# Moving the issue of a small on-chip copy from SyncE's queue to ScalarE's

## The reference, cut to what matters

```
scores = q @ k.T * scale                # per head, 256 x 256, some with a mask or a window
attn   = softmax(scores)                # needs the maximum of each query's scores
out    = attn @ v
```

## Time and profile before

| what | value |
|---|---|
| time, 3 runs | 2492.68 us median (2490.92 to 2495.97) |
| profiled execution | 2494.33 us, of which 2492.2 us is the span |
| granted TensorE clock over the span | 0.983 |
| PE busy | 2363.5 us, 95% of the span |
| ACT busy | 1120.0 us, 45% |
| DVE / POOL busy | 1568.9 us / 517.7 us |

### The profile page before, as it was taken

How to read it: one execution, slowest core, us unless ns; L and a number is a source line. 1 busy time by engine, 2 the same in 40 slices (tenths; PEclk the granted TensorE clock), 3 DMA queues, 4 the chain that set the end, 5 groups by cost and what they waited for, 6 DMA issues and landing times.

```text
span 2492.2 us, 49538 instructions
## 1 busy us (share of the span) xinstructions
PE 2363.5 (95%) x18862; PEld 1745.2 (70%) x18862; DVE 1568.9 (63%) x2673; ACT 1120.0 (45%) x1761; POOL 517.7 (21%) x1120
## 2 busy tenths in 40 slices
PE   6999999999998999999999999999999999999976
PEld 4777777777776676777767677777777677777654
DVE  6757576666757657466675676666665757576422
ACT  3344445544444535435353544444453544545422
POOL 4211113222212222121113122111222212121100
PEclk9999999999999999999999999999999999999987
DMA  7412122321211132212111331121222312211100
GB/s 214 149 39 61 41 64 63 92 64 51 70 49 48 50 83 67 71 53 70 44 53 53 92 85 50 40 74 53 66 71 60 79 48 62 57 49 40 39 18 22
DMA packets 164233, 159.13 MB, mean 64 GB/s; under 512 B 17824, under 2 KB 162720, under 8 KB 162976
## 3 DMA queue, kind: packets, MB, share of 16 engines
q1 hardware_dynamic: 164000, 155.97, 22.9%
HBM read 35.71 MB, written 4.19 MB: 16 GB/s over the span
## 4 chain that ended last, share of the span: by engine, by line
PE 71%; issue 12%; DVE 8%; ACT 3%; DVEq 2%; POOL 2%; POOLq 1%; SPq 1%; DMA 1%; ACTq 0%
PE work L1078 17%; PE work L1069 13%; PE unit L1139 8%; PE out L1161 7%; PE unit L1111 7%; PE unit L1107 5%; PE unit L1135 4%; DVE neg_max L954 4%; PE work L1060 3%; PE work L1276 2%; ACT probs L739 1%; PE unit L1131 1%; PE work L1306 1%; DVE hidden_t L974 1%; DVEq L873 1%
## 5 line engine op out<-in xcount | busy, mean ns | idle before, releaser
L954 DVE TENSOR_REDUCE neg_max<-unit 128x4 f32<-128x1024 f32 (+1 forms) x640 | 727.2, 1163 | 286.6 <-PE unit L1111 281.5
L739 ACT ACTIVATE probs<-unit 128x1024 f32<-128x1024 f32 (+1 forms) x640 | 606.8, 980 | 474.1 <-PE unit L1139 471.2
L1078 PE MATMUL work<-par,hidden_t 128*128 128x256 f32 x1792 | 416.8, 382 | 5.3 <-ACT hidden_t L694 2.2
L1111 PE MATMUL unit<-key_stack,query_stack 96*128 96x256 bf16 x2048 | 350.8, 276 | 23.1 <-issue 8.2
L1078 PEld LDWEIGHTS work<-par,hidden_t 128*128 128x128 f32 x1792 | 332.1, 190 | 55.3 <-ACT hidden_t L694 4.8
L1139 PE MATMUL unit<-query_stack,key_stack 99*128 99x256 bf16 x2048 | 345.7, 276 | 11.0 <-ACT probs L739 4.3
L1069 PE MATMUL work<-tok_t,par 128*128 128x256 f32 x1408 | 335.6, 386 | 3.0 <-ACT tok_t L694 1.9
L1111 PEld LDWEIGHTS unit<-key_stack,query_stack 96*128 96x128 bf16 x2048 | 191.9, 99 | 142.4 <-DVE neg_max L954 23.1
L1069 PEld LDWEIGHTS work<-tok_t,par 128*128 128x128 f32 x1408 | 260.8, 193 | 40.8 <-ACT tok_t L694 4.5
L1161 PE MATMUL out<-probs,values 128*17 128x256 f32 x4096 | 269.2, 386 | 1.2 <-ACT probs L739 1.1
L1139 PEld LDWEIGHTS unit<-query_stack,key_stack 99*128 99x128 bf16 x2048 | 192.5, 98 | 73.9 <-ACT probs L739 14.6
(11 more groups left out here) (163 smaller groups left out, 3293.7 us busy)
## 6 DMA issues: line engine op xcount, KB each, us to landing
query_stack<-query_pieces SPq DMA_DIRECT2D x480, 128.0 KB, 2.4
key_stack<-key_pieces SPq DMA_DIRECT2D x384, 128.0 KB, 2.4
tok_t<-in_x_features SPq DMA_DIRECT2D x16, 256.0 KB, 2.7
c_in<-in_ctx SPq DMA_DIRECT2D x16, 256.0 KB, 3.0
ctx_t<-in_ctx_features SPq DMA_DIRECT2D x16, 256.0 KB, 3.0
x_in<-in_x SPq DMA_DIRECT2D x16, 256.0 KB, 3.2
m_in<-in_mask_self SPq DMA_DIRECT2D x16, 256.0 KB, 3.1
m_in<-in_mask_cross SPq DMA_DIRECT2D x16, 256.0 KB, 3.1
```

The source lines that it names most:

```text
L739: a_.activation(probs[:, n % PROB_BUFS, :, :, 0:width(l)], bank[:, :, :, 0:width(l)], ACT.Exp, scale=SCALE[l]).then_inc(exped, 1)
L954: v.tensor_reduce(neg_max[:, n % HALVES, :, 2 * (u % 4):2 * (u % 4) + 2], bank[:, :, :, 0:width(l)], AX.X, ALU.max, negate=True).then_inc( ...
L1078: last = pe.matmul(bank[:, t, :], src[:, t * P:(t + 1) * P], weight, start=(n == 0), stop=(n == len(parts) - 1))
L1111: last = pe.matmul(bank[:, t, i, 0:n], queries[0:ROWS, h, t * P:(t + 1) * P], keys[0:ROWS, 0 if l == "l2" else h, columns(l, t)], start=ma ...
```

## The change

The `turn` branch of SP's walk is taken out, and the same wait and the same transfer are put into ACT's walk, right behind the cast. The order of the steps is as it was.

```diff
@@ SP's walk
                     if step in ("ksplit", "qsplit"):
                         split(key)
-                    elif step in ("turn0", "turn1"):
-                        n = TURN_NO.place[key]
-                        a = int(step[-1])
-                        wait_taken(sp, key)
-                        sp.dma_start(query_buffer(b, l)[ROWS:MAX_ROWS, HC * a:HC * (a + 1), :],
-                                     max_rows[:, n % 2, :]).then_inc(max_placed[n % 2], 16)
                     elif step == "loadc":
@@ ACT's walk
                         if n >= 2:
                             act.wait_ge(max_placed[n % 2], 16 * (n // 2))
                         a_.copy(max_rows[:, n % 2, :], bank[0:3 * HC, 0, :]).then_inc(taken, 1)
+                        a = int(step[-1])
+                        wait_taken(act, key)
+                        act.dma_start(query_buffer(b, l)[ROWS:MAX_ROWS, HC * a:HC * (a + 1), :],
+                                      max_rows[:, n % 2, :]).then_inc(max_placed[n % 2], 16)
                     elif step == "out0":
```

## The result

The changed kernel takes 2514.6 us (median of 4 runs, 2513.0 to 2515.0) against 2492.4 us before: a ratio of 1.0086, 95% interval 1.0068 to 1.0103, so +22 us (17 to 26). The forecast was 2524 us with a range of 2500 to 2550. In a later comparison the same kernel stood at 1.0085 (1.0072 to 1.0099).

A forecast was written before the change was run, and what follows sets the result against it. PE was taken to bound the kernel, busy for 2363.5 of 2492.2 us. The terms -6 - 1 + 39 - 4 + 2 = +30 us, on the profiled 2494.3 us, gave 2524 us, range 2500 to 2550.

The forecast's parts named there:

- Direction and mechanism: Whole kernel slower: ACT held 0.6 to 1.0 us per issue, half of it on PE; chance 0.65, range 2508 to 2540.
- The price per place: ACT behind each of 160 casts: next instruction 0.85 us after the cast's end, 0.94 us against an overlapped start.
- Signs that were named: Expected in the new trace: ACT issue near 0.74 us, PE's waits for ACT up some 30 us, PE busy near 2363.
- Late copies, -6 and -1 us: SP's queue: copies no longer issued late behind splits gain PE 6 us; splits behind a copy starting earlier gain 1 us.
- What reaches PE, +39 us: ACT's lateness followed to PE's first dependent instruction: 65 of 160 places reach PE by over 0.1 us, 39 us in all.
- the give-back: Part of PE's lateness is recovered where PE later waits for DVE or POOL anyway: -4 us, between 0 and -15.
- Two issuers at once, +2 us: At 41 places ACT might queue behind SP at the shared descriptor generator: 0 to 26 us of ACT's time, +2 us booked.
- The sum: Whole kernel: -6 - 1 + 39 - 4 + 2 = +30 us.
- a cheap issue: Rival: the issue holds ACT under 0.2 us and late copies come home, giving 2486 us; chance 0.07.
- slack that hides all: Rival: gaps on ACT, busy only 45%, take up nearly all of the 39 us, giving 2494 us; chance 0.08.
- a queue behind SP: Rival: ACT queues behind SP's transfers or its issue takes longer than SP's, giving 2537 to 2550 us; chance 0.20.

The follow-up runs named there:

- the extra transfer: Kernel before, SP issuing the real copies, plus an unneeded 12 KB transfer by ACT behind each cast, scratch laid out as the query stack: 1.0090, repeated 1.0095.
- the 65 places: Against the kernel before, ACT issues the copy only at 65 of 160 places where its lateness was read to reach PE; SP issues the rest: 1.0088.
- the other 95: Against the kernel before, ACT issues the copy only at the 95 places where PE was read as not reached; SP issues the rest: 0.9994.
- the first experiment: Kernel before, plus an unneeded 12 KB transfer by ACT behind each cast to plain contiguous scratch rows, issue 0.296 us: 1.0031, +7.7 us.

## Why the prediction was right, and which terms were not

**Direction and mechanism: right.** ACT's issue holds its sequencer as long as SP's; nothing hides it where ACT's next work is ready; PE is not reached at most places. The extra transfer shows it with SP's side left as it was.

**The price per place: right.** 0.85 us was worked out from SP's rows, 0.86 measured at 757.50, and 0.80 to 0.86 at the other places where ACT's next instruction is ready.

**Signs that were named.** ACT's issue has a row of 0.73 us, the exponential at 755 comes 0.86 us behind the cast, PE's wait there is 1.29 us, the copy at 240 is issued 0.03 us behind the cast, and a copy from ACT lands no later: all as forecast. Two signs missed. PE's idle time that ends with ACT grew by 13.2 us and not by some 30, and PE's busy time rose by 7.4 us instead of staying near 2363.

**Late copies, -6 and -1 us: too large.** About -3, an estimate. The term was added up from PE's waits, the smaller of wait and lateness at nine places. The waits went away as forecast: 22.0 us down to 10.2. But those 22.0 were added over PE and PEld, and a wait of both at one place is one wait; PE's rows alone are 3.7 + 2.2 + 1.1 = 7.0 us and 1.2 + 0.7 = 1.9 after. And a wait that goes isn't a time that comes back where something else is late next; at 240 that is ACT itself by way of DVE, as the rows at 240.50 and 242.40 show. For the other places it wasn't followed up.

**What reaches PE, +39 us: too large, and this is the step that failed.** The net of this term and the give-back, 39 - 4, was 35; the extra transfer measures 22 to 24. I put the 18862 matmuls of the trace of before beside those of the changed kernel and took, for each cast, the furthest that any matmul falls back in the 4 us behind it. The sum is 22.5 us at the 65 places and 3.8 us at the other 95; taken at the next cast instead, it is 22.0 and 1.3 us. So at the 65 places nearly nothing was given back up to the next cast (the -4 was too large too); the rest of the 39 us never arrived. Of the 65 places 42 show a fall of over 0.1 us, with sizes as read at many (read 0.85 and 0.87 found at 755, 0.79 and 0.63 at 350), and 23 show none. One such place, before and then after:

```profile
616.37 0.36 ACT L746 CAST max_rows<-work 24x256 bf16<-24x256 f32 x1
...
616.63 1.92 ACT L739 ACTIVATE probs<-unit 128x1024 f32<-128x1024 f32 x2
...
616.96 1.59 PEld L1078 LDWEIGHTS work<-par,hidden_t 128*128 128x128 f32 x8
617.07 1.89 PE L1078 MATMUL work<-par,hidden_t 128*128 128x256 f32 x8
618.89 0.56 PEld L1161 LDWEIGHTS out<-probs,values 128*17 128x17 f32 x16 [0.33 <-issue]
```

```profile
618.00 0.36 ACT L740 CAST max_rows<-work 24x256 bf16<-24x256 f32 x1
...
618.40 0.73 ACTq L743 DMA_DIRECT2D query_stack<-max_rows  x1
...
619.23 1.94 ACT L733 ACTIVATE probs<-unit 128x1024 f32<-128x1024 f32 x2 [0.86 <-ACT max_rows L740]
620.52 0.56 PEld L1159 LDWEIGHTS out<-probs,values 128*17 128x17 f32 x16 [0.33 <-issue]
```

The exponentials start 0.97 us later behind their cast (1.23 against 0.26), and yet PE's `weigh` (L1161, here L1159), which needs the first of them, starts 2.52 us behind the cast both times. In the trace of before PE's sequencer stands at the wait for that exponential at 617.7, while matmuls of L1078 are still running, and I had booked it there with a slack of nil. The wait belongs to the `weigh` at 618.89, so 1.2 us lay between. By my working, 113 waits for exponentials stood beside such a matmul; when they are moved to the step that they belong to, the reading gives 33 us instead of 39. How much of the excess this explains is no more than that reckoning, since no run tested it. The other 11 us, down to the 22, stay open: waits for other counts may stand early in the same way, which was not gone through.

**Two issuers at once, +2 us: nothing seen.** The issue on ACT has a median of 729 ns, and it starts 0.03 us behind the cast at every place. 42 of the 160 overlap an issue of SP's in time, and their median is 729 ns too. Only one is above 0.9 us, the 1.53 us of ACT's first at 31.6. It overlaps issues of SP's, but in the kernel with 65 places ACT's first took 1.34 us with none of SP's beside it, so being ACT's first goes with the long issue and SP need not be there. The Trainium skill, Perfetto Trace Analysis, in its section on the HWDGE DMA instruction says that the descriptor generator is locked by one issuer at a time and that the time of waiting for it would stand in the instruction's row. The trace does not bear out a cost from it here: SP issued its 1084 other transfers beside ACT's 160, and the durations stay as they were (0.600 us for a piece of a split in both traces, in the median).

The sum was +30, the measured +22. What reaches PE less what is given back came out at about 24 instead of 35, the late copies at -3 instead of -7, and two issuers at 0 instead of +2. The errors of 11 and 4 us partly cancelled, so the sum is nearer than its main term; that part is luck. The granted clock wasn't in the sum at all. It doesn't carry the loss: over the timed runs of the extra transfer its mean is within 0.001 of that of the kernel before. The rivals of a cheap issue, of slack that hides all and of a queue behind SP are all refuted, by the rows of L743, the 65 places and the absence of long issues.

## What to carry to other kernels

Price a transfer that is moved to a computing engine at the full time that its sequencer is held, from a row of the same layout, and ask at each place whether that engine's next instruction is ready and who waits for it; the share of busy time says nothing, since 65 issues at tight places cost 22 us and 95 at others nothing that can be told. A wait in PE's stream stands in the trace when the sequencer gets there, which can be over 1 us before the matmuls ahead are through, so measure slack to the first matmul of the step that needs it. Don't book a wait that is removed as time gained, and count a wait that shows on both PE and PEld once.

## What the runs showed of the hardware that was not expected

In these rows the time to issue a transfer goes with its layout more than with its bytes. Of the same 12 KB from 24 partitions: 0.296 us to 24 contiguous pieces in HBM, 0.702 us to 3 rows of 8 pieces in HBM with gaps between the rows, and 0.729 us to the same layout in the stack. Cut in two, with 4 and 8 KB, it takes 0.658 us for each:

```profile
L744 ACTq DMA_DIRECT2D query_stack<-max_rows x320: 642/658/1249, 31.2 to 2521.0; - x160
```

A piece of a split, with eight pieces of 1 KB for each of 16 rows, takes 0.600 us although it moves ten times as much. Why the 3-row layout is dear was not tried; if a layout of the stack let the copy go out in a form as cheap as the one to HBM, which no run shows, ACT would be held 0.4 us per place, and the first experiment says that this costs 8 us.
